# Half of each row tile's transposes moved from TensorE to SyncE's DMA queue in a mixture-of-experts kernel

## What is computed

```python
shared = silu(x_flat @ shared_w1.T) @ shared_w2.T
gate_logits = x_flat @ gate_w.T
top_k_gates, top_k_idx = top_k(gate_logits, 2)          # 8 experts
gates[t, top_k_idx] = softmax(top_k_gates)
h = einsum('td,ehd->teh', x_flat, experts_w1)
expert_out = einsum('teh,edh->ted', silu(h), experts_w2)
out = h_in + shared + einsum('ted,te->td', expert_out, gates)
```

## Time and profile before

| | us |
|---|---|
| median of three runs | 346.7 (346.59 to 347.11) |
| the profiled execution | 347.21 |
| its span in the trace | 345.4 |
| TensorE busy in the span | 319.7 (93%) |
| VectorE / ScalarE / GpSimd busy | 223.5 / 186.9 / 150.1 |

### The profile page before, as it was taken

One profiled execution on the slowest core, in us unless ns is written; L12 is line 12 of the kernel. 1 busy time (PEld: TensorE's weight loads), 2 busy tenths in 40 slices (PEclk: granted clock), 3 DMA queues, 4 the chain that ended last, 5 costly groups with the idle time before them and its releaser, 6 DMA issues.

```text
span 345.4 us, 9654 instructions
## 1 busy us (share of the span) xinstructions
PE 319.7 (93%) x3378; PEld 269.7 (78%) x3378; DVE 223.5 (65%) x497; ACT 186.9 (54%) x407; POOL 150.1 (43%) x224
## 2 busy tenths in 40 slices
PE   7798789999998899799999999999999999999970
PEld 6577678888887698699999777777777877777850
DVE  0235677898878778789988678675655555554530
ACT  1147557778778687666677878762323232323220
POOL 0525556666775234510172154455536353543330
PEclk9989999999999899999999999999999999999995
DMA  7583333324322000491479778233232232323121
GB/s 243 152 266 125 103 102 108 119 80 151 90 85 92 26 27 26 88 347 34 90 197 278 271 217 229 49 63 62 36 60 41 54 47 50 47 47 47 17 32 15
DMA packets 18612, 36.36 MB, mean 105 GB/s; under 512 B 3301, under 2 KB 10952, under 8 KB 18568
## 3 DMA queue, kind: packets, MB, share of 16 engines
q1 hardware_dynamic: 12136, 27.71, 25.2%
q0 software_dynamic: 6432, 8.03, 15.1%
HBM read 28.52 MB, written 7.21 MB: 103 GB/s over the span
## 4 chain that ended last, share of the span: by engine, by line
PE 80%; DVE 8%; POOL 3%; issue 3%; ACT 3%; DMA 1%; SPq 0%; DVEq 0%; ACTq 0%; POOLq 0%
PE bank L744 20%; PE bank L757 13%; PE bank L467 9%; PE bank L557 6%; PE bank L759 6%; PE bank L598 6%; PE bank L492 5%; PE bank L500 3%; PE bank L510 2%; PE bank L546 2%; PE bank L424 2%; PE bank L514 1%; PE bank L668 1%; DVE weights L1207 1%; DVE weights L1216 1%
## 5 line engine op out<-in xcount | busy, mean ns | idle before, releaser
L744 PEld LDWEIGHTS bank<-x_t,weights 128*128 x1248 | 87.4, 98 | 25.6
L744 PE MATMUL bank<-x_t,weights 128*128 128x128 f16 x1248 | 103.9, 219 | 0.0
L920 ACT ACTIVATE act_out<-bank 128x512 f32<-128x512 f32 (+2 forms) x72 | 42.1, 585 | 88.2 <-PE bank L744 75.9
L757 PE MATMUL bank<-weights,hid_hi 128*128 x192 | 73.3, 382 | 0.5
L1143 POOL DMA_INDIRECT out_rows<-y,add_id x26 | 41.7, 1606 | 71.0 <-DVE y L1443 52.7
L1261 DVE SCALAR_TENSOR_TENSOR hid_lo<-act_out,hid_hi 128x512 f16<-128x512 f32 (+2 forms) x72 | 48.6, 680 | 13.1 <-ACT hid_hi L931 11.6
L759 PE MATMUL bank<-weights,hid_lo 128*128 x192 | 52.3, 273 | 0.0
L1267 DVE SCALAR_TENSOR_TENSOR weights<-stage,weights 128x1024 f16<-128x1024 f32 x36 | 42.9, 1216 | 0.4 <-ACT weights L884 0.2
L1070 POOL TENSOR_SCALAR weights<-weights 111x1 f32<-111x1 f32 x22 | 14.4, 655 | 57.1 <-DVE weights L1169 57.0
L884 ACT ACTIVATE weights<-stage 128x1024 f16<-128x1024 f32 x36 | 36.8, 1047 | 0.0
L467 PE MATMUL bank<-weights 128*111 128x256 f32 x132 | 34.1, 411 | 2.3 <-ACT weights L832 1.0
(11 more groups left out here) (142 smaller groups left out, 548.7 us busy)
## 6 DMA issues: line engine op xcount, KB each, us to landing
stage<-in_w_ffn SPq DMA_DIRECT2D x36, 512.0 KB
weights<-in_patches SPq DMA_DIRECT2D x11, 333.0 KB, 3.2
x_rows<-rows SPq DMA_DIRECT2D x11, 111.0 KB
out_rows<-weights SPq DMA_DIRECT2D x10, 111.0 KB
out_rows<-y POOLq DMA_DIRECT2D x9, 119.0 KB, 5.8
weights<-in_w_embed SPq DMA_DIRECT2D x3, 256.0 KB, 4.7
weights<-in_w_qk SPq DMA_DIRECT2D x1, 512.0 KB, 5.8
slot_rows<-x_rows,gather_id POOLq DMA_INDIRECT x26, 3.8
```

Of the source, the lines that this page charges most:

```text
L744: mm = nc.tensor.matmul(o, weights[:, bass.ds(base + 2 * k * CHUNK + 2 * (col - col % D) + w * D + col % D, P)], x_t[:, b, (2 * x + k) * P ...
L757: nc.tensor.matmul(bank[5 + b][0:m, :], hid_hi[:, b, c * P:c * P + m], weights[:, bass.ds(at, 2 * D)], start=(c == 0), stop=False)
L920: nc.scalar.activation(d_, s_, ACT.Silu, scale=1.0 / (X_SCALE * W_SCALE)).then_inc(hid_acted, 1)
```

## The change

The two high quarters of each slot are now turned by two transposing transfers on SyncE's queue, straight from `slot_rows` to `x_t`. TensorE turns the other two, and ScalarE copies half as much. `turn_slot(0)` and `turn_slot(1)` stand behind the load of chunk 25; `turn_slot(j)` for j of 2 to 6 stands behind two more loads each. A turn waits for the gathered rows and, from slot 2 on, until the matmuls of slot j - 2 no longer read that half of `x_t`. TensorE waits for the transfers at the start of each slot, and GpSimd before it gathers into the same rows again.

```diff
+AHEAD = 26
+DMA_TURNS = 2
...
-            for c in range(FRONT_CHUNKS + DRAIN_CHUNKS, NCHUNK):
+            def turn_slot(j):
+
+                sp.wait_ge(slot_rows_in[j % 4], 16 * (j // 4 + 1))
+                if j >= 2:
+                    sp.wait_ge(hid_ready, 2 * (UNITS + j) - 2)
+                for q in range(DMA_TURNS):
+                    sp.dma_start(x_t[:, j % 2, q * P:(q + 1) * P], slot_rows[:, j % 4, q * P:(q + 1) * P],
+                                 transpose=True).then_inc(x_t_in[j % 2], 16)
+
+            for c in range(FRONT_CHUNKS + DRAIN_CHUNKS, AHEAD):
                 load_chunk(c)
+            turn_slot(0)
+            turn_slot(1)
+            for j in range(2, SLOT_TILES):
+                for c in range(AHEAD + 2 * (j - 2), min(AHEAD + 2 * (j - 1), NCHUNK)):
+                    load_chunk(c)
+                turn_slot(j)
...
-                for q in range(4):
+                for q in range(DMA_TURNS, 4):
...
                 pe.wait_ge(x_t_ready, 1)
+                pe.wait_ge(x_t_in[0], DMA_TURNS * 16)
...
                 pe.wait_ge(x_t_ready, j + 1)
+                pe.wait_ge(x_t_in[b], DMA_TURNS * 16 * (j // 2 + 1))
...
-                v_ = bank[4][:].bitcast(F16)[:, 0:4 * P]
-                nc.scalar.copy(x_t[:, j % 2], v_).then_inc(x_t_ready, 1)
+                v_ = bank[4][:].bitcast(F16)[:, DMA_TURNS * P:4 * P]
+                nc.scalar.copy(x_t[:, j % 2, DMA_TURNS * P:], v_).then_inc(x_t_ready, 1)
...
                     pool.wait_ge(x_turned, j - 3)
+                    pool.wait_ge(x_t_in[j % 2], DMA_TURNS * 16 * ((j - 4) // 2 + 1))
```

More of the change, by code:

```diff
@@ L256, in build @@
         slot_rows_in = [sem(f"slot_rows_in{i}") for i in range(4)]
+        x_t_in = [sem(f"x_t_in{i}") for i in range(2)]
         x_turned = sem("x_turned")
```

## The result

The changed kernel takes 361.7 us (median of four, 360.1 to 362.1) beside 346.9 us for the kernel before, a ratio of 1.042 with a 95% interval of 1.040 to 1.045. Forecast were 353.6 us and a range up to 360.0: the direction was right, but the loss is 14.8 us where I had 6.9.

A forecast was written before the change was run, and what follows sets the result against it. TensorE was taken as the bound in the slots. Terms -2.9 (transposes), +7.4 (stall), +1.7 (clock) and +0.65 (waits) summed to +6.9 us, from 346.7 to 353.6 us; range 349.5 to 360 us.

The forecast's parts named there:

- The bound: From 200 us on, where the 26 slots run, TensorE was claimed the bound: busy 29.75 and 30.00 of 30 us.
- Removed transposes: Two fewer TensorE transposes in each slot, 52 in all at 0.056 us each, were to save 2.9 us.
- is not covered by them in particular: The register load after a slot's transposes was claimed to be covered by as many other queued instructions, not specially by transposes.
- The stall at slot 0: TensorE waits for slot 0's transfers, issued behind load 25, until 190.0: +7.4 us, bounds 5.5 and 10.3.
- 1.05 MB take 4.2 us, to 188.5: Loads 24 and 25, ahead of slot 0's transfers, were to move at 251 GB/s from 184.33 and finish at 188.5.
- The 1.5 us for the pair behind the loads: Slot 0's two small transfers were estimated to land 1.5 us after the loads ahead, at 190.0.
- The clock: The pause before slot 0 lets TensorE's clock fall: 3.4 us at half clock, +1.7 us, between 0 and 1.9.
- The wait at each start: 19 more wait instructions at slot starts: 17 at 0.03 us and 0.14 for slot 8, +0.65 us.
- Rival A: The extra wait instruction costs 0.15 us in each of 18 slots, +2.7 us, time 355.7 us; chance 18%.
- The reading of the three slots: First down-matmul pieces of slots 7, 8 and 14 were read as: first wait instruction about 0.01 us, second 0.14.
- A pair in 3.5 us, so it fits: From slot 2 on, two transposing transfers take about 3.5 us of the 5.98 us available, so they cost 0.
- rival B: Pairs slower than 5.98 us from release make each of 24 slots wait; at 7.6 us, time 392 us; chance 13%.

## Why the prediction was wrong

**The bound.** Right. TensorE's time is the kernel's time in the slots. What the views had not told apart is TensorE computing and TensorE's queue issuing: a row that says "busy 30.00 of 30 us" reads the same for both, as a drained pipeline hides in the modelled length of a matmul.

**Removed transposes, -2.9 us.** Wrong, and the largest term besides the stall. Measured with two transposes fewer: -0.010 us for each late slot, some -0.3 us in all. The step that failed is the sentence that the register load "is not covered by them in particular". I had argued with the number of queued instructions; the traces show that 0.46 us pass from the load's start to the next down matmul, with four transposes or two, and the transposes run within them. The hint was in the profile: the first piece behind the transposes takes 0.31 to 0.33 us where others take 0.22.

**The stall at slot 0, +7.4 us.** The mechanism was right in each step, down to load 25 (forecast 185.46, measured 184.93) and the transfers right behind it. The size was 10.05 us, within the bounds of 5.5 and 10.3, but not at the value taken. The step that was mis-sized is "1.05 MB take 4.2 us, to 188.5": load 25 landed at 191.1, 6.2 us after its issue, where the forecast had 3.0. It counted only the bytes of loads 24 and 25, as if the full DMA engines had nothing else to move; the trace of the kernel before had single loads of up to 6.3 us, and the engines still full (share 0.98) from 189.0 to 191.4. The 1.5 us for the pair behind the loads were rather too much: it landed 0.8 us behind load 25.

**The clock, +1.7 us.** Right in kind, a little over its bound of 1.9: 2.1 us measured as the rest of slot 0's 12.2, from 4.3 us at half clock instead of 3.4.

**The wait at each start, +0.65 us.** Mis-sized: one more wait and nothing else gives 0.083 a slot, 1.3 us in the 16 late ones and some 1.5 in all. Rival A had 2.7. The reading of the three slots was too fine: it told that waits differ in price, but not what one costs at the start. The price is 0 once the load is gone, so it isn't one of the wait alone; that it depends on how far the queue is ahead is my reading.

**A pair in 3.5 us, so it fits, 0.** Half right. Alone it takes 3.6 to 5.4 us and fits; those waited for among the weight loads took 6.6 to 8.8, which is a part of rival B. Behind slot 0 only 1.0 us of that shows in the changed kernel, at slot 5, where the gather was late too; without the stall at slot 0 it shows at two slots, 2 and 5.

**The sum.** Forecast +6.9. Stall +2.65 more, clock +0.4, transposes +2.6 not won, waits +0.85, slot 5 +1.0: +14.4, against +14.7 in the spans. The late slots alone leave 0.3 us (1.45 less 1.33 for the wait, plus 0.16 for the transposes), the 0.3 that transfers with nobody waiting also add there. The range failed for the same reason as the sum: each of its ends took the full 2.9 us of the transposes for granted. With that bounded by 0 the high end, 360 and 2.9, would have held the 361.7.

**What a transfer costs.** The Trainium skill's 1309 ns for a transpose by DMA ("VectorE: DVE Perf Modes", "The three transpose paths") is near the 1.1 to 1.3 us for which one occupies SyncE's queue here, but is no latency: a pair landed 3.6 us after its release at best. That a queue's descriptors are consumed in ring order (the Trainium skill, "DMA: Bandwidth & Descriptors", "Queues, rings and completion order") agrees with the pairs that landed 0.8 us behind the load ahead, at 191.93 and 196.15. Where the Trainium skill's page "Advanced Engine Details and Errata", section "X-Bar Transpose (TRN2)", says that these transfers are as fast as regular ones, no run here bears it out for 32 KB.

## What to carry to other kernels

Before work is taken off a saturated TensorE, ask whether it is the matmuls or something in its queue that fills the time: what runs while a register load holds up the next matmul may give nothing when it is removed, while the load and one more wait show. Such loads go to a place with constant addresses, which here won 3.1 us. A transfer that replaces a few hundred ns of TensorE needs several us from release to landing, more beside bulk loads, and is placed by what stands ahead of it in its queue, not by what it reads.

## What the runs showed of the hardware

- A transposing transfer of 128x128 half-precision numbers, 32 KB from SBUF to SBUF, is 160 packets, all under 512 B, and mostly takes 1.1 to 1.3 us to issue (up to 2.2 us in the changed kernel), against 0.33 us for a plain load of 512 KB.
- Two of them land 3.6 us after their release with little other traffic, 5.2 us beside a gather, and 6.6 to 8.8 us where TensorE waited for them among 512 KB loads; behind load 25 that is 0.8 us after the load's own landing.
- A register load of 0.30 us in TensorE's queue cost 0.146 us a slot among matmuls with computed addresses: 0.46 us pass from its start to the next such matmul, with four transposes between or two. Among matmuls with constant addresses 26 of them cost nothing that can be told from the scatter of the traces.
- A wait that was met long before cost 0.083 us at a slot's start, and nothing once the register load was gone.
- Two transposes fewer were worth 0.111 us without the load, 0.010 us with it.
